# Encoder units and causal batches as straight code, expert numbers packed into words, a new order inside the unit

## The reference

```python
x = x + masked_attention(layernorm(x), ctx, ctx, mask)             # one head, 16 batches
x = x + moe_encoder(layernorm(x))                                  # below
x = x + causal_attention(layernorm(x), ctx, ctx)                   # 16 heads of 16
x = x + shared_and_top1_experts(layernorm(x))                      # 8 small experts, 512 tokens

def moe_encoder(x):                                                # 4 experts, the best 2 for each batch
    logits = x.mean(axis=1) @ gate_w.T + gate_b
    top = top_k(logits, 2); weight = softmax(logits)
    # each expert is an encoder layer: q/k/v projection, attention of 16 heads, output projection,
    # x1 = layernorm(x + o); layernorm(x1 + relu(x1 @ l1w.T + l1b) @ l2w.T + l2b)
    return sum(weight[b, e] * encoder_layer_e(x[b]) for e in top[b])
```

## Time and profile before

| | |
|---|---|
| median of 3 runs | 860.69 us (855.89 to 861.27) |
| profiled execution: time, span | 861.79 us, 860.0 us |
| mean granted TensorE clock | 0.912 of full speed |
| busy, share of the span: PE | 737.0 us, 86% |
| DVE | 633.1 us, 74% |
| ACT | 347.5 us, 40% |
| POOL | 378.0 us, 44% |
| chain that ended last | PE 71%, DVE 14%, issue 8%, POOL 4% |

### The profile page before, as it was taken

One profiled execution on the slowest core, in us unless ns is written; L12 is line 12 of the kernel. 1 busy time (PEld: TensorE's weight loads), 2 busy tenths in 40 slices (PEclk: granted clock), 3 DMA queues, 4 the chain that ended last, 5 costly groups with the idle time before them and its releaser, 6 DMA issues.

```text
span 860.0 us, 29844 instructions
## 1 busy us (share of the span) xinstructions
PE 737.0 (86%) x10976; PEld 587.0 (68%) x10977; DVE 633.1 (74%) x1856; ACT 347.5 (40%) x710; POOL 378.0 (44%) x648
## 2 busy tenths in 40 slices
PE   6699659999999999999999999998788898734885
PEld 5588547787878778877878787885565566422663
DVE  3686556776777777777777777879889999845865
ACT  3655324434343434434443434444344455321210
POOL 1788613444444445353544445342334454335132
PEclk9755579999999999999999999999999999965797
DMA  7677400000000000000000000001312212112000
GB/s 263 215 219 237 150 2 2 3 2 1 0 0 0 0 0 0 0 0 0 0 0 0 0 2 2 16 21 58 99 56 74 85 59 83 51 59 88 14 1 7
DMA packets 24581, 40.19 MB, mean 47 GB/s; under 512 B 3725, under 2 KB 16663, under 8 KB 24265
## 3 DMA queue, kind: packets, MB, share of 16 engines
q1 hardware_dynamic: 23096, 37.38, 13.2%
q0 software_dynamic: 704, 1.71, 0.7%
q10 hardware_dynamic: 722, 0.28, 0.1%
HBM read 30.84 MB, written 8.91 MB: 46 GB/s over the span
## 4 chain that ended last, share of the span: by engine, by line
PE 71%; DVE 14%; issue 8%; POOL 4%; ACT 3%; DMA 1%; POOLq 0%; ACTq 0%; SPq 0%; DVEq 0%
PE ps L466 7%; PE ps L460 7%; PE ps L661 6%; PE ps L468 6%; PE ps L467 6%; PE ps L643 5%; DVE mx L1412 4%; PE ps L593 4%; PE ps L699 3%; PE ps L701 3%; PE ps L700 3%; PE ps L595 3%; PE ps L594 2%; PE ps L585 2%; PE ps L697 2%
## 5 line engine op out<-in xcount | busy, mean ns | idle before, releaser
L1819 POOL TENSOR_TENSOR rs<-mv,cst 128x1 f32<-128x1 f32 x132 | 28.9, 219 | 339.9 <-DVE mv L1190 302.8
L1412 DVE TENSOR_REDUCE mx<-ps 128x16 f32<-128x2048 f32 x48 | 109.8, 2287 | 1.6 <-PE ps L616 1.6
L1046 ACT ACTIVATE pT<-ps 128x1024 f32<-128x1024 f32 x96 | 93.0, 1021 | 32.2 <-PE ps L643 30.1
L699 PE MATMUL ps<-xh,w_hi 128*128 128x128 bf16 x512 | 100.1, 220 | 0.0
L700 PE MATMUL ps<-xl,w_hi 128*128 128x128 bf16 x512 | 99.9, 219 | 0.0
L701 PE MATMUL ps<-xh,w_lo 128*128 128x128 bf16 x512 | 99.9, 219 | 0.0
L1821 POOL TENSOR_TENSOR rs<-rs,cst 128x1 f32<-128x1 f32 x132 | 74.2, 562 | 10.3
L466 PE MATMUL ps<-w_hi,hh 128*128 x256 | 70.1, 274 | 0.0
L468 PE MATMUL ps<-w_lo,hh 128*128 x256 | 69.8, 273 | 0.0
L467 PE MATMUL ps<-w_hi,hl 128*128 x256 | 69.8, 273 | 0.0
L593 PE MATMUL ps<-ycT_hi,w_hi 128*128 128x128 bf16 x256 | 59.4, 232 | 0.0
(11 more groups left out here) (363 smaller groups left out, 2528.9 us busy)
## 6 DMA issues: line engine op xcount, KB each, us to landing
stage<-in_w SPq DMA_DIRECT2D x32, 384.0 KB, 3.7
vec<-in_vec SPq DMA_DIRECT2D x4, 896.0 KB, 5.8
vec<-in_tw SPq DMA_DIRECT2D x12, 256.0 KB, 2.8
ctxc<-in_ctx SPq DMA_DIRECT2D x19, 128.0 KB, 2.1
comb<-x SPq DMA_DIRECT2D x16, 128.0 KB, 1.7
comb<-t SPq DMA_DIRECT2D x16, 128.0 KB, 1.8
shared<-x1b SPq DMA_DIRECT2D x16, 128.0 KB, 1.7
out<-x SPq DMA_DIRECT2D x16, 128.0 KB, 1.8
```

The costliest lines, as they stand in the source:

```text
L699: mm(dst, w(w_hi, c, j), xh[:, c, :], start=False, stop=False)
L1046: A(pT[:, 8 * a:8 * a + 8, :].rearrange("p h q -> p (h q)"), ps[:, 2 * a:2 * a + 2, :].rearrange("p g k -> p (g k)"), ACT.Exp, scale=SCALE ...
L1412: nc.vector.tensor_reduce(mx[:, :], att.rearrange("p g s k -> p (g s) k"), AX.X, ALU.max, negate=True).then_inc(m_max, 1)
```

## The change

1. The loops of the encoder and of the causal stage are gone on PE, ACT, DVE and POOL: all blocks are written out. SP keeps its loop.
2. DVE packs the numbers of 8 units into one int32 (`words`, digits of base 4). Each engine loads a word every 8 blocks and takes a unit's number out with a shift and a mask. PE starts the encoder stage on `g_words`.
3. PE's order in a block: `projection_qk` is taken one block ahead, between `out_proj` and `scores_T`; `second` runs its half 1 first, ahead of `values`, and half 0 behind `x1_transposes`; `o_rows` stands behind it; `prep` moves up behind `scores`; `o_transposes` stands between the two halves of `hidden`.
4. DVE, ACT and POOL are put in an order that fits: `stats1` right behind `sum1`, `h_low` in the block of its `hidden`, `y_of` early, `norm2` behind `sum2`, `shift_split` ahead of `o_low`; ACT's `oo` behind `relu(f, 1)`; POOL's bias sums ahead of `affine1`, the root of the second norm behind it.
5. `t2` gets a second buffer (`t2s`), in free columns of `h`.

```diff
+        t2s = (h[:, 256:512], t2[:, :])
+        words = sb("words", [128, UNITS // WORD], i32)
...
+        def word_of(engine, g):
+            return engine.value_load(words[0:1, ds(g, 1)], min_val=0, max_val=4 ** WORD - 1)
+        def digit(word, k):
+            return (word >> (2 * k)) & 3
...
@@ tensor: second @@
-                pe.wait_ge(hl_b if half else hl_a, u + 1)
+                if half == 1:
+                    pe.wait_ge(hl_b, u + 1)
+                    pe.wait_ge(hl_a, u + 1)
...
@@ tensor: block @@
-                projection_qk(km, base_m, e_m)
                 if not isinstance(m, int) or m > 2:
                     pe.wait_ge(hl_b, m - 2)
-                projection_v(base_m)
+                projection_v(None if causal_m else ex(1)[0])
+                if encodes(g):
+                    second(g, 1, ex(-2)[0])
                 if attends(n):
                     values(n, slot, 0)
                     values(n, slot, 1)
-                if encodes(g):
-                    second(g, 0, ex(-2)[0])
-                if attends(n):
-                    o_rows(n)
                 if encodes(f):
                     pe.wait_ge(v_sb, m + 1)
                     x1_transposes(f)
                 if encodes(g):
-                    second(g, 1, ex(-2)[0])
+                    second(g, 0, ex(-2)[0])
+                if fetch is not None:
+                    fetch()
+                if attends(n):
+                    o_rows(n)
                 scores(m, causal_m)
+                if kp is not None:
+                    pe.wait_ge(qk_split, m + 1)
+                    prep(kp, isinstance(kp, int) and kp >= B)
+                if encodes(f):
+                    hidden(f, 1, *ex(-1))
                 if attends(n):
                     o_transposes(n)
                 if encodes(f):
-                    hidden(f, 1, *ex(-1))
                     hidden(f, 0, *ex(-1))
-                if fetch is not None:
-                    fetch()
                 shift_transpose(m)
                 if attends(n):
                     out_proj(n, None if causal_n else ex(0)[0])
-                if kp is not None:
+                if next_k is not None:
                     pe.wait_ge(qk_split, m + 1)
-                    prep(kp, isinstance(kp, int) and kp >= B)
+                    base, e = (None, E) if causal(n + 2) else ex(2)
+                    projection_qk(next_k, base, e)
                 scores_T(m, causal_m)
...
@@ tensor: the calls @@
-            pe.wait_ge(g_ready, 1)
+            pe.wait_ge(g_words, 1)
...
+            projection_qk(0, *ex_of(0))
+            for n in range(-1, UNITS + 1):
+                if n == UNITS - 2:
                     pe.wait_ge(wc_ready, 1)
+                fetch = n % WORD == WORD - 4 and n // WORD + 1 < UNITS // WORD
+                block(n, n % 2, lambda j: ex_of(n + j), prep_of(n + 2), batch_of(n + 2) if n < UNITS else None,
+                      (lambda: words_pe.append(word_of(pe, n // WORD + 1))) if fetch else None)
+            for b in range(1, B + 4):
+                block_c(b, b % 2, ex_of(UNITS - 1)[0] if b == 1 else None)
...
@@ vector: the words, behind g_ready @@
+            digits = gl[:, 6, 0:UNITS].rearrange("p (g k) -> p g k", k=WORD)
+            g_link(tt(digits, chosen[:, :].rearrange("p (g k) -> p g k", k=WORD),
+                      cst[:, C_POW:C_POW + WORD].rearrange("p (o k) -> p o k", o=1).broadcast_to(
+                          [128, UNITS // WORD, WORD]), ALU.mult))
+            g_link(nc.vector.tensor_reduce(gs[:, 7, 0:UNITS // WORD], digits, AX.X, ALU.add))
+            cp(words[:, :], gs[:, 7, 0:UNITS // WORD]).then_inc(g_words, 1)
...
@@ gpsimd: block @@
-                if encodes(n - 3):
-                    rstd(2, n - 2, l2_var, l2_veps, l2_rstd)
                 if encodes(f):
                     rstd(1, n, l1_var, l1_veps, l1_rstd)
                 if kp is not None:
                     y_root(kp)
+                if causal(m):
+                    x_bias(m - UNITS, 1 - slot)
+                else:
+                    y_bias(m, km, 1 - slot, ex(1))
                 if encodes(f):
                     affine1(f, ex(-1))
                     x1_bias(f, 1 - slot, ex(-1))
                 if encodes(n - 3):
+                    rstd(2, n - 2, l2_var, l2_veps, l2_rstd)
                     affine2(n - 3, ex(-3))
```

More of the change, by code:

```diff
@@ L1532, in block @@
                         sum1(n, slot)
[L1533 to L1534 removed]
+                        stats1(n)
+                if encodes(f):
+                    h_low(f, 0)
+                if encodes(g):
+                    stats2(g, slot)
+                if ks is not None:
+                    y_stats_of(at(ks[1]), ks[0])
             def stats_c(b):
```

218 lines of the change are left out of this document (61 added, 157 removed).

## The result

The changed kernel takes 838.8 us (median of 4 runs, 836.56 to 840.94), the kernel before 860.02 in the same session: ratio 0.975, 95% interval 0.972 to 0.979. I had said 837, with a range of 822 to 854. The sum was right, but several of its terms were not: one had the wrong sign, two were too small by more than half, one came to nothing, and the errors cancel.

What follows compares the result with a forecast made beforehand. PE was taken to bound the encoder units, with DVE fullest in the causal stage. 861.8 - 21.1 - 1.9 + 2 - 6.4 + 4.8 + 1.6 - 2.5 = 838.3, less 1.1 to the median: 837 us, range 822 to 854.

Steps and rivals of the forecast that it cites:

- Loops and expert loads: PE's issue waits at loads and loops go, -21.1; hidden length of twelve gaps, -1.9; remaining word loads, +2 us.
- the 1.2 at L661: Longer of two issue waits at values, assigned to the encoder loop's end and counted as removed, 1.2 us.
- The three later word loads: PE's word loads behind second's first-run half, outside the ramp, 0.36 to 1.10 us each, taken as 0.7: +2 in all.
- q/k ahead of scores_T: Moved behind out_proj, the q/k projection gets 0.2 us shorter in each of 32 units: -6.4, bounds 0 to -16.
- the sequencer enters with some lead: At the q/k projection: out_proj's six 256-column matmuls run longer than their issue, so up to 0.5 us a unit is saved.
- The late feedforward chain: POOL's affine steps late for PE's x1 transposes by 0.3 us in 16 even blocks: +4.8, between 0 and +24.
- Rival 1: PE's sequencer is never late, q/k takes 1.57 us and no new waits come: 821 us, chance 0.17.
- out_proj waits for oo_split: Chain of maxima, shift_split, o_low ahead of out_proj is 0.1 us late in 16 blocks without prep: +1.6, 0 to 5.
- The second buffer: Two buffers for sum2 let norm2 stand behind it; neither was waited for before, so 0.
- Causal stage: Only the loop goes; its entry wait and part of a 4.2 us loss come back: -2.5, from -0.9 to -4.2.
- The contention of POOL with the gate product: Causal stage: POOL's expert-weight split slows DVE's gate product from 0.28 to 1.21 us; by the skill's rule it stays.
- Rival 3: Straight code arrives late: some 64 more instruction packets, each holding PE up 0.93 us, +60, 897 us; chance 0.03.

Runs made afterwards that it cites:

- experiment 2: The changed kernel with the q/k projection put back behind scores_T, all else in the new order: 835.8 us, ratio 0.974 to the kernel before.
- experiment 5: The changed kernel with o_low ahead of shift_split, y_low ahead of norm2, the shift transpose behind out_proj, relu of half 0 ahead of ACT's shift copy: 836.3 us.
- experiment 3: Changed kernel variants: q/k at constant addresses 831.1 us, all PE expert addresses constant 826.7, q/k behind twelve wide products 839.2, q/k alternating with quarters of values 869.5.
- experiment 6: The changed kernel with one buffer for the second residual sum, so norm2 stands ahead of sum2 again: 842.8 us, ratio 0.983 to the kernel before.
- experiment 4: Kernel before with only the causal stage written out: 857.7 us; the same with PE's code shifted by padding: 857.1; changed kernel with causal loops back: 843.2.

## Why the prediction was right, step by step

- **Loops and expert loads, -21.1 - 1.9 + 2.** The core of it, and right: 19.3 by the kernel that has only the straight code and the words (units 2 to 30). One reading was false: the 1.2 at L661 isn't the encoder loop's end. It stands at 754.62 in the tail of the causal stage, and after has it still (1.18 at 731.39). That the longest of two waits had no row of its own should have made me look at its time. Without it the term is -19.8. The three later word loads cost 0.4 together and not 2: from the last matmul of `second` to the scores it is 0.76, 0.76 and 0.82, where the other blocks have 0.64. In the kernel with the order of before the same load stands ahead of the q/k projection, and PE is idle for 0.42 to 0.45 there.
- **q/k ahead of scores_T, -6.4.** Wrong in sign: the place costs 1.8 (experiment 2). The row (2.07 where the pitch would give 1.57) was read rightly, and constant addresses do give 1.65. The step that failed is "the sequencer enters with some lead": behind `out_proj` the projection takes 2.18 plus a gap, as long as behind `scores_T`. `out_proj` has computed addresses of its own, and a shift and a mask are computed behind it; which of these uses up the lead isn't shown. Even twelve wide products leave a lead for only eleven matmuls. The new order costs 3.1 in units 2 to 30 where my terms gave -6.4 + 4.8 + 1.6 = 0. With the wait for `oo_split` taken out (experiment 5) it is 1.1 better than the old one (368.0 and 369.1).
- **The late feedforward chain, +4.8.** 0 in after, 12.2 in the kernel with a fast q/k projection. Place, engine and the 16 even blocks were right. The slip is that I took q/k at 2.07 in this term and at 0.2 less in the one before. The gain did not come, so neither did the loss of its cover. The two terms were one, with a sum near zero for small shifts; that saved the forecast. Rival 1 (821) needed both a fast projection and no new wait, and experiment 3 shows that the first brings the second: even then it was 831.
- **out_proj waits for oo_split, +1.6.** Place and kind were right, the size was too small: 0.23 in every second unit, some 3.7; experiment 5 takes 4.3 out.
- **The second buffer, 0.** About 2 us of use, by experiment 6.
- **Causal stage, -2.5.** It is -6.1, and not by the mechanism I named. The loop's entry costs nothing that can be seen, its blocks 0.2 each. The rest, 4.7, is a standstill in `values` with what follows from it. It is absent in after, and small (one interval of 13.3) where the encoder units are straight code in the old order. I bounded the term by a loss of 4.2 in two blocks, measured against 12.42. That is a looped block itself: against the 12.14 of a straight one the two blocks lose 4.7, and the looped blocks behind them 1.4. The contention of POOL with the gate product, which I expected to stay, is small in after: it takes 0.35 to 0.42 (L1547) in the blocks of the expert weights and 1.00 in the last two.
- **Rival 3, fetches.** Instruction packets rose from 41 to 96 on their main queue, and no "issue" wait above 0.3 came with them in the encoder stage. The Trainium skill (Runtime: NRT & Kernel Launch, Instruction fetch mechanics) says that going from one block of code to the next is mostly hidden, and the encoder stage agrees. Its sentence on taken branches does not explain the 0.93, with which I had paired it: the standstill comes without a loop there, too. If it is a late fetch, which experiment 4 leaves likely but not shown, this rival's mechanism was at work in the kernel before and not in the straight code.

The errors, measured less predicted: loads and loops -19.3 for -21.0, +1.7; the order 3.1 for 0, +3.1; the causal stage -6.1 for -2.5, -3.6; and -0.9 in stretches that I had left at 0. They cancel to 0.3 us (-23.2 for -23.5). The range held, but with more luck than the single steps deserve.

## What to carry to other kernels

Sum the waits that a change removes from the rows, and cost a reordering as one term: what a stretch of work gains by moving and what it covered at its old place are the same microseconds, and can't be booked separately. Before an "issue" row is given to a loop or a load, look at its time and at the instructions on both sides; one in the middle of a run of equal matmuls belongs to neither. When code is padded to move it, count what the padding really adds: here each matmul was two instructions. And when computed addresses slow a run of short matmuls, judge the place by how many instructions with constant addresses stand ahead; then shorten it only if the engine that delivers next has the slack.

## What the runs showed of the hardware

- Three word loads behind wide matmuls cost PE 0.12 to 0.18 us each, the same load behind `scores_T` 0.42 to 0.45 of idle time, a single load at the unit's start 0.27 to 0.39, two numbers with what follows 1.3 (263.78 to 265.10).
- Matmuls of 128 columns with computed weight addresses started 0.056 us apart in the hidden layer and behind quarters of `values`, and 0.07 to 0.08 apart (2.06 to 2.18 for 28) behind `out_proj` and behind `scores_T`. With constant addresses it is 0.059 (1.66 / 28) there. That the sequencer's lead makes the difference is the reading that fits all of these.
- Going from bf16 matmuls of the q/k projection to float32 matmuls of `values` and back cost some 0.4 us each time, with no wait in the list (one kernel, experiment 3).
- A wait of 2.1 us of PE is followed by the 1.2 GHz level in some profiles and by full clock in others, with the same instructions around it; it cost 1.6 us at the end of the causal stage.
- In the masked stage the granted clock ranged from 0.50 to 1.00 (60 to 90 us) from profile to profile, and the stage was not shorter at 1.00: of the fourteen, the two profiles at full clock had the latest unit 2 (146.5).
- Not settled: what holds PE for 0.9 to 1.2 us in the middle of 16 matmuls in causal block 4, when the encoder units run in a loop. PE went on 1.30 to 1.34 us behind the landing of an instruction packet in all three.
